# Mixer of a two-layer block: the part carried between chunks made feature-major, C times the decay rows multiplied with the states straight into the output's bank, tanh in place

## The reference, cut to what matters

```python
H_, P_, N_, G_, K_, CH_ = (64, 64, 128, 1, 4, 32)
INTER = H_ * P_                                    # 4096
proj = input_states @ in_proj_w.T
gate, hBC, dt = jnp.split(proj, [INTER, INTER + CONV_DIM], axis=-1)
x = hBC.transpose(0, 2, 1)
x = jax.lax.conv_general_dilated(x, conv_w, (1,), [(K_ - 1, 0)], ...)
hBC = jax.nn.silu((x + conv_b[None, :, None]).transpose(0, 2, 1))
hs, Bmat, Cmat = jnp.split(hBC, [INTER, INTER + G_ * N_], axis=-1)
...
A_cum = jnp.cumsum(Ac, axis=-1)
L = jnp.exp(segsum(Ac))
Gm = jnp.einsum('bclhn,bcshn->bclsh', Cc, Bc)
M = Gm * L.transpose(0, 2, 3, 4, 1)
Y_diag = jnp.einsum('bclsh,bcshp->bclhp', M, xc)
states = jnp.einsum('bclhn,bhcl,bclhp->bchpn', Bc, decay_states, xc)
...
state_decay = jnp.exp(A_cum)
Y_off = jnp.einsum('bclhn,bchpn,bhcl->bclhp', Cc, states, state_decay)
y = (Y_diag + Y_off).reshape(b, s, H_, P_) + D_res
yg = y * jax.nn.silu(gate)
var = jnp.mean(yg * yg, axis=-1, keepdims=True)
return (norm_w * (yg * jax.lax.rsqrt(var + EPS))) @ out_proj_w.T
```

## Time and profile before

| | us |
|---|---|
| median of 3 runs (2288.8 to 2296.66) | 2289.03 |
| span of the profiled execution | 2334.2 |
| PE busy | 1987.9 (85%) |
| DVE busy | 1699.9 (73%) |
| ACT busy | 1458.4 (62%) |
| POOL busy | 974.3 (42%) |

### The profile page before, as it was taken

How to read it: one execution, slowest core, us unless ns; L and a number is a source line. 1 busy time by engine, 2 the same in 40 slices (tenths; PEclk the granted TensorE clock), 3 DMA queues, 4 the chain that set the end, 5 groups by cost and what they waited for, 6 DMA issues and landing times.

```text
span 2334.2 us, 41032 instructions
## 1 busy us (share of the span) xinstructions
PE 1987.9 (85%) x12211; PEld 1614.9 (69%) x12211; DVE 1699.9 (73%) x3913; ACT 1458.4 (62%) x3983; POOL 974.3 (42%) x1025
## 2 busy tenths in 40 slices
PE   4787878787788468999999998999989996879995
PEld 4566666666566256888787887778877885557772
DVE  4676767766533577999889998999989997734444
ACT  1474747474133157888887888878887886235550
POOL 0120303030266112454454765556654666175551
PEclk8799999998699779999999999999999998979998
DMA  4047473839522404544353554445534552745547
GB/s 130 28 163 301 148 306 127 345 120 370 205 87 86 145 10 136 159 147 158 110 169 128 168 176 141 141 145 178 167 134 138 167 168 88 222 123 155 160 143 268
DMA packets 148070, 376.87 MB, mean 161 GB/s; under 512 B 22640, under 2 KB 72176, under 8 KB 145552
## 3 DMA queue, kind: packets, MB, share of 16 engines
q1 hardware_dynamic: 132640, 332.58, 41.8%
q0 software_dynamic: 15216, 41.67, 5.3%
HBM read 234.81 MB, written 139.37 MB: 160 GB/s over the span
## 4 chain that ended last, share of the span: by engine, by line
PE 55%; DVE 17%; ACT 14%; issue 6%; DMA 3%; another core or an unknown queue 2%; SPq 1%; POOL 1%; DVEq 0%; POOLq 0%; ACTq 0%
PE bank L2158 11%; PE bank L2214 6%; ACT work L702 5%; PE bank L2604 4%; PE bank L2186 4%; DVE cv L2325 3%; PE bank L2207 3%; PE bank L2199 3%; PE bank L2641 2%; ACT l_mat L2249 2%; PE bank L2172 2%; DVE nmax L608 2%; PE bank L1075 2%; PE bank L1104 2%
## 5 line engine op out<-in xcount | busy, mean ns | idle before, releaser
L2158 PE MATMUL bank<-h_hi,wi 128*128 128x512 f32 x1024 | 403.6, 435 | 1.3 <-ACTq L152 1.3
L2249 ACT ACTIVATE l_mat<-l_mat,cum_tok 128x128 f32<-128x128 f32 x1024 | 315.1, 424 | 0.0
L2325 DVE SCALAR_TENSOR_TENSOR cv<-bank,cw,cv 128x511 f32<-128x511 f32 (+2 forms) x384 | 287.4, 748 | 32.1 <-ACT cv L2255 13.5
L2378 POOL TENSOR_TENSOR xdec<-xdt,dec_tok 128x384 f32<-128x384 f32 x128 | 107.8, 842 | 387.4 <-DVE xdt L2315 354.2
L2393 POOL TENSOR_TENSOR yg<-yd,sgt 128x512 f32<-128x512 f32 x128 | 227.2, 1775 | 45.6 <-DVE yd L2332 45.6
L2214 PE MATMUL bank<-wo,yg 128*128 128x256 f32 x1024 | 242.4, 380 | 1.5 <-POOL yg L2393 1.5
L2158 PEld LDWEIGHTS bank<-h_hi,wi 128*128 128x128 f32 x1024 | 195.4, 191 | 62.1 <-issue 23.7
L2158 PE MATMUL bank<-h_lo,wi 128*128 128x512 f32 x512 | 203.2, 397 | 0.0
L2214 PEld LDWEIGHTS bank<-wo,yg 128*128 128x128 f32 x1024 | 184.8, 190 | 21.8 <-POOL yg L2393 1.9
L2386 POOL TENSOR_TENSOR gates<-gates,sq 128x512 f32<-128x512 f32 x128 | 164.2, 1283 | 71.9 <-ACT sq L2266 71.8
L846 POOL CAST w_hi<-w_raw 128x512 fp32r<-128x512 f32 x32 | 21.1, 659 | 382.0 <-ACTq L152 232.3
(11 more groups left out here) (417 smaller groups left out, 4937.1 us busy)
## 6 DMA issues: line engine op xcount, KB each, us to landing
sorted_rows<-blank SPq DMA_DIRECT2D x16, 4644.0 KB, 31.7
wi<-in_weights_split SPq DMA_DIRECT2D x128, 512.0 KB
l_mat<-running_sums SPq DMA_DIRECT2D x128, 512.0 KB, 4.9
experts_got<-chosen_rows SPq DMA_DIRECT2D x32, 512.0 KB, 9.3
wo<-out_weights_normed SPq DMA_DIRECT2D x128, 128.0 KB
experts_xt<-sorted_rows SPq DMA_DIRECT2D x127, 129.0 KB
w_raw<-in_wi SPq DMA_DIRECT2D x32, 256.0 KB, 2.6
in_weights_split<-w_hi SPq DMA_DIRECT2D x32, 256.0 KB, 2.9
```

Of the source, the lines that this page charges most:

```text
L2158: mm = e.matmul(dst[:, :], l, r[:, k, tok], start=(n == 0), stop=(n == 3 * KD - 1))
L2249: last = e.activation(part, part, ACT.Relu, bias=cum_tok[:, c, hh, bass.ds(w.g, 1)], scale=-1.0)
L2325: e.scalar_tensor_tensor(out=cv[:, w.two, n:SEQ], in0=PSX[w.two][:, 0:SEQ - n], scalar=cw[:, bass.ds(w.f, 1), TAPS - 1 - n], in1=cv[:, w.t ...
```

## The change

The states of the chunks are no longer multiplied with C, evacuated with a scale and transposed. Instead the decay is put on C before the matmul, in feature-major layout. ACT takes the exponential of the loaded row of running sums of tile n-1 (columns 128 to 511 of both heads) into the new tile `ce`, before the Relu instructions overwrite that row. POOL multiplies `ce` with `c_t`. PE multiplies the states (64 columns of a head as weights) with `ce` straight into the bank `PY`, six matmuls behind the eight of the within-chunk part. The three `L2207` matmuls, the six evacuations, the three transposes of `y_off`, the tiles `y_off`, `e_tok` and the bank `PO` go. The copy of the first chunk's state moves from DVE to ACT. The two tanh write straight into `xc` and `sgt` and `thx` and `thg` go. New waits come with it, as the diff shows.

```diff
@@ mixer_pe_step
         w = tiles[1]
         if w.live:
             e.wait_ge(s_xc, done(w.g))
-            e.wait_ge(s_st, done(w.g - 1, 3))
+            e.wait_ge(s_st, done(w.g - 1, 2))
...
         if w.live:
             e.wait_ge(s_m, done(w.g))
             e.wait_ge(s_xdt, done(w.g))
-            e.wait_ge(s_offs, done(w.g))
+            e.wait_ge(s_ce, done(w.g))
+            e.wait_ge(s_st, done(w.g, 2))
             e.wait_ge(s_yd, done(w.g - 1))
-            for c in range(1, NC):
-                e.matmul(PY[:, c * P:(c + 1) * P], y_off[:, c - 1, :], ident[:, :], is_transpose=True, start=(c == 1),
-                         stop=False, skip_group_check=True)
             for c in range(NC):
                 for hh in range(2):
                     rows = slice(hh * SSM_P, (hh + 1) * SSM_P)
-                    mm = e.matmul(PY[rows, c * P:(c + 1) * P], xdt[:, w.four, c, rows],
-                                  m_mat[:, w.two, hh, c * P:(c + 1) * P], start=False, stop=(c == NC - 1),
+                    e.matmul(PY[rows, c * P:(c + 1) * P], xdt[:, w.four, c, rows],
+                             m_mat[:, w.two, hh, c * P:(c + 1) * P], start=(c == 0), stop=False,
+                             skip_group_check=True)
+            for c in range(1, NC):
+                for hh in range(2):
+                    rows = slice(hh * SSM_P, (hh + 1) * SSM_P)
+                    mm = e.matmul(PY[rows, c * P:(c + 1) * P], st[:, w.two, c - 1, rows],
+                                  ce[:, w.two, hh, (c - 1) * P:c * P], start=False, stop=(c == NC - 1),
                                   skip_group_check=True)
             mm.then_inc(s_y, 1)
...
-        w = tiles[2]
+        w = tiles[0]
         if w.live:
-            e.wait_ge(s_st, done(w.g, 3))
-            e.wait_ge(s_offs, done(w.g - 1))
+            e.wait_ge(s_cv, done(w.g))
             route("p")
-            for c in range(NC - 1):
-                mm = e.matmul(PO[:, c * P:(c + 1) * P], c_t[:, w.b, c, :], st[:, w.two, c, :], start=True, stop=True)
-            mm.then_inc(s_off, 1)
@@ mixer_act_step
-        w = tiles[3]
+        w = tiles[2]
         if w.live:
-            e.wait_ge(s_off, done(w.g))
-            route("a")
-            e.wait_ge(s_y, done(w.g - 1))
-            for c in range(NC - 1):
-                for hh in range(2):
-                    rows = slice(hh * SSM_P, (hh + 1) * SSM_P)
-                    last = e.activation(y_off[:, c, rows], PO[:, c * P + hh * SSM_P:c * P + (hh + 1) * SSM_P],
-                                        ACT.Identity, scale=e_tok[:, c, hh, bass.ds(w.g, 1)])
-            last.then_inc(s_offs, 1)
+            e.wait_ge(s_ss, done(w.g))
+            e.wait_ge(s_y, done(w.g - 2))
+            e.activation(st[:, w.two, 0, :], PT[:, 0:P], ACT.Copy).then_inc(s_first, 1)
+        route("a")
         w = tiles[1]
         if w.live:
             e.wait_ge(s_lb[w.four], 16 + w.loaded_i)
+            e.wait_ge(s_y, done(w.g - 2))
+            e.activation(ce[:, w.two, :, :], l_mat[:, w.four, :, P:SEQ], ACT.Exp).then_inc(s_e, 1)
+            e.wait_ge(s_e, done(w.g))
             for hh in range(2):
                 for c in range(NC):
...
             e.wait_ge(s_tap, done(w.g, 3))
-            e.wait_ge(s_xc, done(w.g - 1))
-            e.activation(thx[:, :], cv[:, w.two, :], ACT.Tanh, scale=0.5).then_inc(s_thx, 1)
+            e.wait_ge(s_yd, done(w.g - U))
+            e.activation(xc[:, w.four, :], cv[:, w.two, :], ACT.Tanh, scale=0.5).then_inc(s_thx, 1)
...
-            e.wait_ge(s_sg, done(w.g - 1))
-            e.activation(thg[:, :], PSZ[:, :], ACT.Tanh, scale=0.5).then_inc(s_thz, 1)
+            e.wait_ge(s_yg, done(w.g - U))
+            e.activation(sgt[:, w.four, :], PSZ[:, :], ACT.Tanh, scale=0.5).then_inc(s_thz, 1)
@@ mixer_dve_step
         w = tiles[2]
         if w.live:
             e.wait_ge(s_ss, done(w.g))
+            e.wait_ge(s_first, done(w.g))
             route("a")
-            e.wait_ge(s_off, done(w.g - 2))
-            e.tensor_copy(st[:, w.two, 0, :], PT[:, 0:P]).then_inc(s_st, 1)
             for c in (1, 2):
...
-            e.scalar_tensor_tensor(out=xc[:, w.four, :], in0=thx[:, :], scalar=1.0, in1=cv[:, w.two, :],
+            e.scalar_tensor_tensor(out=xc[:, w.four, :], in0=xc[:, w.four, :], scalar=1.0, in1=cv[:, w.two, :],
@@ mixer_pool_step
         e = q.e
+        w = tiles[2]
+        if w.live:
+            e.wait_ge(s_e, done(w.g))
+            e.tensor_tensor(ce[:, w.two, :, :], ce[:, w.two, :, :],
+                            c_t[:, w.b, :, :].rearrange("p c l -> p (c l)").unsqueeze(1).broadcast_to([P, 2, SEQ - P]),
+                            ALU.mult).then_inc(s_ce, 1)
         w = tiles[1]
```

More of the change, by code:

```diff
@@ L1409, in program @@
     dec_tok = sb("dec_tok", [P, NC - 1, 2, NB], where=mix)
-    e_tok = sb("e_tok", [P, NC - 1, 2, NB], where=mix)
     e_in = sb("e_in", [P, 2, NB, NC - 1], where=mix)
@@ L1438, in program @@
     st = sb("st", [P, 2, NC - 1, P], where=stream)
-    y_off = sb("y_off", [P, NC - 1, P], where=stream)
+    ce = sb("ce", [P, 2, 2, SEQ - P], where=stream)
     yd = sb("yd", [P, SEQ], where=stream)
@@ L1868, in exponents @@
                          ACT.Exp).then_inc(g_out, 1)
-            e.activation(e_tok[:, :, :, :], cum_tok[:, 1:NC, :, :], ACT.Exp)
             e.activation(dec_tok[:, :, :, :], dec_tok[:, :, :, :], ACT.Exp)
@@ L2029, in start_pool @@
                                 ALU.subtract).then_inc(p_low, 1)
[L2032 removed]
+    (s_x, s_z, s_e, s_diff, s_cv, s_tap, s_thx, s_thz, s_xc, s_sg, s_l, s_m, s_t, s_xdt, s_xdec, s_ss, s_first, s_st, s_ce,
      s_y, s_yd, s_yg, s_sq, s_acc, s_o) = [sem("mix_" + n) for n in (
[L2034 to L2035 removed]
+         "x", "z", "decay_rows", "sum_diffs", "conv_first", "taps", "tanh_x", "tanh_z", "x_conv", "silu_z", "decay_mat", "m_mat",
+         "x_turned", "x_dt", "x_decayed", "state_sums", "first_state", "states", "c_decayed", "y", "y_skip", "y_gated",
          "squares", "squares_summed", "out")]
@@ L2342, in mixer_dve_step @@
             e.wait_ge(s_thz, done(w.g))
-            e.wait_ge(s_yg, done(w.g - U))
-            e.scalar_tensor_tensor(out=sgt[:, w.four, :], in0=thg[:, :], scalar=1.0, in1=PSZ[:, :],
+            e.scalar_tensor_tensor(out=sgt[:, w.four, :], in0=sgt[:, w.four, :], scalar=1.0, in1=PSZ[:, :],
                                    op0=ALU.add, op1=ALU.mult).then_inc(s_sg, 1)
@@ L2404, in mixer_pe @@
     def mixer_pe(t):
-        for s in (s_x, s_z, s_t, s_ss, s_off, s_y, s_o):
+        for s in (s_x, s_z, s_t, s_ss, s_y, s_o):
             t.e.drain().then_inc(s, BACK)
@@ L2412, in mixer_act @@
     def mixer_act(a):
-        for s in (s_cv, s_thx, s_thz, s_diff, s_l, s_sq, s_offs):
+        for s in (s_cv, s_thx, s_thz, s_e, s_diff, s_l, s_sq, s_first):
             a.e.drain().then_inc(s, BACK)
@@ L2429, in mixer_pool @@
     def mixer_pool(q):
-        for s in (s_xdec, s_yg, s_acc):
+        for s in (s_xdec, s_ce, s_yg, s_acc):
             q.e.drain().then_inc(s, BACK)
```

10 lines of the change are left out of this document (3 added, 7 removed).

## The result

| | before | after |
|---|---|---|
| median, run beside each other (4 runs each) | 2290.85 us (2288.8 to 2296.66) | 2979.52 us (2967.12 to 2985.79) |
| ratio, 95% interval | | 1.2963 (1.2930 to 1.2995) |
| span of the profiled execution | 2334.2 us | 2975.4 us |
| first to last first tap of the mixer | 1061.6 us | 1731.0 us |

Forecast were 2973 us and a range of 2780 to 3060. The mixer's own 127 intervals, which answer to the earlier trace rows, became 669.4 us longer, of the 688.7 between the medians.

What follows compares the result with a forecast made beforehand. It took PE's queue and an equally long ACT and DVE round, 7.83 us a step, as the bound. Closed round 513, drain 6 and clock 165 sum to 684 us; on 2289 that is 2973 us, range 2780 to 3060.

Steps and rivals of the forecast that it cites:

- The ring: Mixer step: ACT's Exp waits for y, closing a round over PE, ACT and DVE; 11.87 us a step, 513 us more.
- The clock: PE, idle twice a step, drops to its lower clock on transposes and y; 165 us, bounds 0 to 279.
- The 67 us of group ends and routing: Mixer time beyond 127 intervals of 7.83 us; DVE's routing pieces lie on the ring, so this was left unchanged.
- the third rival: Mixer round does not close, copy and Exp cheaper: ACT round 7.70 us, 2272 us, 0.7% faster; chance 0.02.
- The drain: End of the mixer: the last tiles run out through lengthened steps; 6 us, bounds 0 and 16.
- The span: Whole profiled execution: 3018 us, taking its 45 us over the median of before as unchanged.
- The full clock: Rival in the mixer: the round closes but PE's clock stays full; 2808 us, chance 0.26.
- The open round: Rivals where y is there when ACT asks: 2290 us, no change (0.03), or 2272, 0.7% faster (0.02).

Runs made afterwards that it cites:

- The wait alone: Kernel before plus only ACT's wait, ahead of the Relu of tile n-1, for the y of tile n-3: 2763.57 us, ratio 1.2005.
- the filled versions: Kernel after with 16 unread matmuls a step in PE's idle stretches: 2888.35 us; the same with POOL's product of ce and C behind xdec: 2834.66 us.
- the product late: POOL's product of ce and C moved behind xdec: on the kernel after 2961.21 us, with PE also kept busy by unread matmuls 2834.66 us.
- the split version: Kernel after with ACT's Exp into its own two-buffer tile; POOL makes a single ce behind xdec and waits for y instead: 2415.56 us, ratio 1.0333.
- the version through PSUM: The split version with ACT's tanh of x written into the x projection's PSUM bank, read there by DVE's xc product: 2301.32 us, ratio 1.0009.

## Why the prediction was right, and where it was not

**The ring.** Forecast 11.87 us a step, measured 11.78. All ten links are within 0.05 us of the forecast; the largest miss is y with the way to ACT, 1.86 for 1.91. The idle times it named are there: ACT 4.12 ahead of the Exp, PE 1.60 (forecast 2.0) and 1.94 (2.3). The term, forecast 513 us, is 503 by the measured step (127 x 3.96). The wait alone and the filled versions show it from both sides: without the new work the step is 10.90, and without the clock's share it is 11.79. One reading ahead of the sum is off: the y that ACT waits for before `y_off` is that of the tile before, so of one step back and not two. Nothing in the sum uses it.

**The clock** was the mis-sized term. Forecast were 165 us: low stretches in three steps of four, 1.7 us each. That the clock falls, where (on the transposes and y) and by how much at the most (13.4 - 11.8 = 1.6) was right. Over the steps 5 to 34 the mean loss was 12.81 - 11.78 = 1.03 us, against 1.3, and over the 88 intervals outside the routed ones it was 70 us, against 88 x 1.3 = 114. Filling PE gained 85 us in all, and 131 with the product late. Neither is the whole share of the clock, as the routed intervals keep some of the lower clock in both, and the 85 have paid 11 for the filling. The gaps at which it fell are those of the timeline above, 1.94 and 1.60 us. The Trainium skill, TensorE: Matmul & The Clock Gate, on a second failure mode, describes a clock that oscillates with short, frequent idle stretches; the trace agrees, with 1.00 and 0.83 in windows next to each other and y at 1.68 us in one step and 3.14 in the next. The Trainium skill, on the same page, in its section on why this matters for your kernels, warns only of idle gaps longer than these; by that the clock would have stayed full, and here that was too lenient.

**"The 67 us of group ends and routing are not absorbed, and I leave them as they are"** is the step that failed. The 39 routed intervals became 251 us longer, 97 more than their 39 x 3.96 = 154 of ring, where the forecast has 39 x 1.3 = 51 for the clock and nothing else. With PE filled they are still 76 over the ring, and with the product late as well 31. The 44 between the two (before rounding) are mostly POOL's product against DVE's routing pieces. The 31 left are the longer norm and routing at the group ends and the lower clock there, whose shares no run tells apart. The prediction asked whether the product fits into POOL's idle time. It does in the steady steps; over the whole kernel PE waited 26 times, 27 us together, for the `xdec` that stands behind it. What it left out is that POOL's work can make DVE's longer. The Trainium skill, SBUF — State Buffer, in the section on two separate sides, states that VectorE with two SBUF inputs and GpSimd take one pair of ports in turn, and that the later one waits for the whole instruction of the other. The runs agree: `outs` 1.22 became 2.57, and `xc` went back from 1.98 on average to 0.69 when one of its inputs was in PSUM. At the prices of these runs it would have raised the sum of the forecast by 30 us (the product late, in the routed intervals of the kernel after) to 44 us (the same with PE filled). It bears more on the third rival, as the split version shows.

The two errors nearly cancel. Forecast for the mixer were 513 + 114 + 51 = 678 us, for the ring, the 88 intervals and the 39. Measured are 503 + 70 + 97, which is 669 before rounding. That the total came so much closer than its parts is luck.

**The drain** (6 us) was right: from the last first tap to the end of the last out projection it takes 23.3 us before and 30.4 after, 7.2 more. The other 12 of the 19 us outside the intervals can't be told from what varies there: the runs of the kernel before on one chip differ by up to 22 us.

**The span** forecast, 3018, was wrong by 43 us. It took the 45 us of the profiled execution of before as a property of the kernel. They lie outside the mixer and came with every run on one of the chips.

**The rivals.** The full clock (2808) has its likeness in the two filled versions, at 2835 and 2888. The open round, forecast as no change or 0.7% faster, is the split version: it came out 3.3% slower, mostly because `xc` ran into POOL. That its mechanism is sound, the version through PSUM shows: there the ring over ACT and DVE is 7.55 us, less than the 7.70 forecast, and PE, busy throughout, does its queue in it, for which the forecast had 7.61. But POOL's own queue took the gain in the scatter steps until these were spread.

## What to carry to other kernels

Before a wait is put on an in-order engine, follow what stands behind it until the chain comes back to what it waits for. If it closes within one step, the period is the sum of the links, however idle every engine looks. A tile made by one engine, changed by a second and read by a third can be freed late only by the last reader; a buffer between the first two lets the second one do the waiting. And an engine with room in its queue still isn't free work where its instruction shares SBUF with DVE's: ask which inputs each has, and whether one of them could lie in PSUM.

## What the runs showed of the hardware

- A DVE instruction with two SBUF inputs and a POOL product hold each other up, in whichever order they start. DVE second: `outs` 2.57 for 1.22, `xc` 1.58 behind one instruction of POOL and 3.30 behind three in a row, for 0.69. POOL second: `yg` 1.78 for 1.29, and a copy of one column 1.20 behind `outs` where it else takes 0.19. With one input in PSUM `xc` took 0.69 beside `ce` and `gates`.
- Whether DVE gets its turn between two POOL instructions that follow each other closely differs. In the split version `xc` at 1050.70 waited for `gates` only, and `yg` behind it had to wait; `xc` at 1339.16 waited for `ce`, `gates` and `yg`. What decides it no run shows.
- With two idle gaps of 1.60 and 1.94 us in each step, PE kept going to the lower of its clock's two levels, 1.2 GHz, and back to 2.4; with the same waits and the gaps filled the granted clock of the steady steps was 1.00.
